# L0 attention of a four-stage kernel: projections moved by half a batch in four pieces, group sums in one bank pair, quantising in two parts, new first loads

## What is computed

```python
x = x + tanh(g_xattn[0]) * L0_xattn(layernorm(x), ctx, ctx)     # causal, 16 heads of 32, no weights
x = x + tanh(g_ffn[0])   * L0_ffn(layernorm(x), w_gate_up, w_proj)
x = x + tanh(g_xattn[1]) * L1_xattn(layernorm(x), ctx, ...)     # its keys and values: ctx @ k_w + k_b, ctx @ v_w + v_b
x = x + tanh(g_ffn[1])   * L1_ffn(layernorm(x), ...)
# L0_ffn's weights, in groups of 64:
scale = clip(mean(abs(w)), 1e-8); w_hat = clip(round(w / scale), -1, 1) * scale
# L1_ffn's weights: one scale for each matrix, from the mean of abs(w)
```

## Time and profile before

| | us |
|---|---|
| median of 3 runs | 1223.16 (1221.94 to 1225.69) |
| the profiled execution's own time | 1224.48 |
| its span | 1222.7 |
| TensorE busy in the span | 1131.6 (93%) |
| VectorE, ScalarE, GpSimd busy | 832.7, 567.3, 72.8 |

### The profile page before, as it was taken

One profiled execution on the slowest core, in us unless ns is written; L12 is line 12 of the kernel. 1 busy time (PEld: TensorE's weight loads), 2 busy tenths in 40 slices (PEclk: granted clock), 3 DMA queues, 4 the chain that ended last, 5 costly groups with the idle time before them and its releaser, 6 DMA issues.

```text
span 1222.7 us, 23942 instructions
## 1 busy us (share of the span) xinstructions
PE 1131.6 (93%) x9578; PEld 689.9 (56%) x9672; DVE 832.7 (68%) x1440; ACT 567.3 (46%) x918; POOL 72.8 (6%) x180
## 2 busy tenths in 40 slices
PE   4998999898989999999999897999999999999998
PEld 2555555555567777777777554545454545454543
DVE  5577767765756765755665545778787878777785
ACT  4655565656333332333333333336373737372644
POOL 0000000000000000000000010110101010101010
PEclk8999999999999999999999998999999999999999
DMA  9345434541131101111101020010101010100000
GB/s 359 125 132 174 156 121 130 166 147 61 44 121 53 51 29 36 53 35 35 53 18 35 18 78 23 15 35 2 52 2 52 2 52 2 35 10 10 10 9 35
DMA packets 28974, 78.75 MB, mean 64 GB/s; under 512 B 3009, under 2 KB 3137, under 8 KB 28481
## 3 DMA queue, kind: packets, MB, share of 16 engines
q1 hardware_dynamic: 28864, 77.22, 19.4%
HBM read 64.63 MB, written 12.58 MB: 63 GB/s over the span
## 4 chain that ended last, share of the span: by engine, by line
PE 84%; DVE 6%; ACT 4%; issue 4%; DMA 0%; POOL 0%; SPq 0%; ACTq 0%; DVEq 0%; POOLq 0%
PE bank L507 9%; PE bank L601 9%; PE bank L602 9%; PE bank L636 9%; PE bank L616 9%; PE bank L739 7%; PE bank L727 5%; PE bank L405 5%; PE bank L769 4%; PE bank L689 2%; PE bank L708 2%; PE bank L445 2%; ACT ARENA L965 2%; PE bank L466 2%; PE bank L421 2%
## 5 line engine op out<-in xcount | busy, mean ns | idle before, releaser
L601 PE MATMUL bank<-ARENA,W 128*128 128x256 f16 x1024 | 227.9, 273 | 0.9 <-issue 0.9
L602 PE MATMUL bank<-ARENA,W 128*128 128x256 f16 x1024 | 227.8, 273 | 0.0
L934 ACT ACTIVATE ARENA<-bank 128x512 f32<-128x512 f32 (+3 forms) x143 | 93.0, 687 | 107.0 <-PE bank L405 34.0
L739 PE MATMUL bank<-W,ARENA 128*128 128x512 bf16 x493 | 117.2, 383 | 4.7 <-ACT ARENA L934 2.2
L616 PE MATMUL bank<-W,ARENA 128*128 128x512 bf16 x472 | 116.3, 383 | 3.2 <-DVE ARENA L1347 0.9
L507 PE MATMUL bank<-ARENA 128*128 128x512 f32 x256 | 117.2, 602 | 0.0
L636 PE MATMUL bank<-ARENA 128*128 128x512 f32 x256 | 116.8, 599 | 0.0
L601 PEld LDWEIGHTS bank<-ARENA,W 128*128 128x128 bf16 x1024 | 100.4, 98 | 19.5 <-issue 1.3
L602 PEld LDWEIGHTS bank<-ARENA,W 128*128 128x128 bf16 x1024 | 100.5, 98 | 18.6 <-issue 0.3
L1486 DVE SCALAR_TENSOR_TENSOR ARENA<-bank,ARENA 128x512 f32<-128x512 f32 x64 | 48.0, 750 | 86.5 <-PE bank L602 86.5
L934 ACT ACTIVATE ARENA<-ARENA 128x512 f16<-128x512 f32 x64 | 40.3, 629 | 133.9 <-DVE ARENA L1486 131.1
(11 more groups left out here) (178 smaller groups left out, 1784.8 us busy)
## 6 DMA issues: line engine op xcount, KB each, us to landing
W<-in_w SPq DMA_DIRECT2D x48, 512.0 KB, 3.8
ARENA<-in_w SPq DMA_DIRECT2D x24, 512.0 KB, 3.6
kv_store<-ARENA SPq DMA_DIRECT2D x32, 256.0 KB, 2.2
W<-kv_store SPq DMA_DIRECT2D x15, 512.0 KB, 4.5
X<-in_x SPq DMA_DIRECT2D x8, 512.0 KB, 4.7
ARENA<-in_ctxT SPq DMA_DIRECT2D x8, 512.0 KB, 3.8
ARENA<-in_ctx SPq DMA_DIRECT2D x8, 512.0 KB, 6.1
out<-X SPq DMA_DIRECT2D x16, 256.0 KB, 2.9
```

The source lines that it names most:

```text
L601: pe.matmul(bank[:, i * S:(i + 1) * S], W0[:, at:at + P], xt_half(b, 0)[:, k, :], start=(k == 0), stop=False)
L602: mm = pe.matmul(bank[:, i * S:(i + 1) * S], W0[:, at:at + P], xt_half(b, 1)[:, k, :], start=False, stop=(k == KD - 1))
L739: mm = pe.matmul(to, bufC["QQ"][:, t, k * P:(k + 1) * P], W1[:, at:at + D], start=(k == 0), stop=(k == KD - 1))
L934: return act.activation(to, src, ACT.Copy)
```

## The change

Stage A is put in another order; no operation of the computation is dropped or added. Names as before; the new line numbers are some 3 to 20 higher.

- Key pieces 0 and 1 of batch f are made in the turn before that of the batch's attention, one after `a_turn_x(f)` and one between the last two `a_probs`; value pieces 2 and 3 stand after the first `a_scores` and after the second group sum's place in the batch's own turn. Turn 0 becomes a short lead-in of its own, with both key pieces of batch 0. Banks: `bank_of_kv` is 4, 1, 6, 7.
- The first group sum of a batch stays in the turn before, the second and third are in the batch's turn, all in banks 2 and 3.
- `a_quantise` becomes `a_distance` (four operations) and `a_ternary` (two, with the maximum). The first unit is quantised whole between the maxima of scores 0 and of scores 1; unit 1 has other work between its parts.
- In the last turn the first half of `b_gate_up(0, 0)` stands between the last two `a_probs`, the other half after `m_weights`.
- The first loads are `cst`, x, keys, `gate`, `cols`, then the key weights; `selq` and `selc` get a semaphore of their own and are copied after `split_row`. Stores of pieces 0 and 1 are issued at the end of the turn before.

```diff
-        kv = [[(f"kv{i}", s.a_kvr, 4, i, late)] for i in range(4)]
-        gs = [("gs0", s.a_s, 3, 0, 0), ("gs1", s.a_s, 3, 1, 0), ("gs2", s.a_s, 3, 2, late)]
+        kv = [[(f"kv{i}", s.a_kvr, 4, i, late * (i // 2))] for i in range(4)]
+        gs = [("gs0", s.a_s, 3, 0, 0), ("gs1", s.a_s, 3, 1, late), ("gs2", s.a_s, 3, 2, late)]
...
+        bank_of_kv = (4, 1, 6, 7)
...
+            sp.dma_start(pre["cst"], cst).then_inc(s.ld_cst, 16)
             load_x(0)
-            sp.dma_start(pre["cst"], cst).then_inc(s.ld_cst, 16)
-            sp.dma_start(pre["selq"], selq).then_inc(s.ld_cst, 16)
-            sp.dma_start(pre["selc"], selc).then_inc(s.ld_cst, 16)
+            load_keys(0)
             sp.dma_start(keep["gate"], gates).then_inc(s.ld_cst, 16)
             sp.dma_start(keep["cols"], cols).then_inc(s.ld_cst, 16)
-            load_keys(0)
+            sp.dma_start(bufA["wkv"][:, 0, :], wkv[:, 0:KD * D]).then_inc(s.ld_wk, 16)
+            sp.dma_start(bufA["tmp"][:, 0, :], vec[:, 0:D]).then_inc(s.ld_kb, 16)
             load_w0(0)
+            sp.dma_start(pre["selq"], selq).then_inc(s.ld_sel, 16)
+            sp.dma_start(pre["selc"], selc).then_inc(s.ld_sel, 16)
+            sp.dma_start(bufA["wkv"][:, 1, :], wkv[:, KD * D:2 * KD * D]).then_inc(s.ld_wv, 16)
...
+            a_project(0, 0, 0)
+            a_turn_x(0, 0)
+            a_group_sum(0, 0, 0)
+            a_project(0, 0, 1)
...
             for turn in range(NB + 1):
...
                 if back:
                     a_scores(b, 0)
+                    a_distance(b, 0)
+                    a_ternary(b, 0)
+                    a_scores(b, 1)
+                    a_max_parts(b, 0)
...
                     a_scores(b, 2)
-                    a_quantise(b, 1)
+                    a_distance(b, 1)
                 if end:
                     a_divide(e)
                 if back:
                     a_scores(b, 3)
                     a_max_parts(b, 1)
+                    a_ternary(b, 1)
                     if not front:
                         b_turn_x(0)
                     a_max_rows(b, 1)
-                    a_quantise(b, 2)
+                    a_distance(b, 2)
+                    a_ternary(b, 2)
```

More of the change, by code:

```diff
@@ L350, in sync_program @@
                 load_w0(3 * turn + 4)
[L351 to L352 removed]
+                if f < NB:
+                    store_kv(f, 0)
+                    store_kv(f, 1)
                 load_keys(turn + 1)
@@ L501, in a_project @@
                 what, t = i // TB, i % TB
-                bank = banks[(6, 7, 4, 5)[i]]
+                bank = banks[bank_of_kv[i]]
                 W = bufA["wkv"][:, what, :].rearrange("p (k d) -> p k d", k=KD)
-                pe.wait_ge(s.ld_wkv, 32)
-                pe.wait_ge(*ringA[(6, 7, 4, 5)[i]].freed(f"kv{i}", turn))
+                pe.wait_ge((s.ld_wk, s.ld_wv)[what], 16)
+                pe.wait_ge((s.ld_kt0, s.ld_kt1)[b % 2], 16 * (b // 2 + 1))
+                pe.wait_ge(*ringA[bank_of_kv[i]].freed(f"kv{i}", turn))
                 for k in range(KD):
@@ L531, in b_turn_x, with b_gate_up @@
                     turned(to, [bufB["xn"][:, t, k * P:(k + 1) * P] for k in range(KD)], keep["identf"]).then_inc(s.b_xt, 1)
-            for turn in range(NB + 1):
+            def b_gate_up(b, p, parts=(0, 1)):
+                q, first = 8 * b + p, 2 * ((p + 1) % 2)
+                if p == 0:
+                    pe.wait_ge(s.b_xl, 2 * b + 2)
+                if q == 0:
+                    pe.wait_ge(s.a_r, 16)
+                    pe.wait_ge(s.a_scr, 4 * NB)
+                if q == 1:
+                    pe.wait_ge(s.m_scl, 1)
+                    pe.wait_ge(s.a_otr, 3 * NB - 2)
+                pe.wait_ge(s.b_sg, max(0, q - 1))
+                pe.wait_ge(s.b_h, max(0, q - 1))
+                for part_ in parts:
+                    bank, col, done = banks[first + part_], part_ * HID + 2 * p * P, (s.b_g, s.b_gu)[part_]
+                    for i in range(2):
+                        for k in range(KD):
+                            at = k * 2 * HID + col + i * P
+                            pe.matmul(bank[:, i * S:(i + 1) * S], W0[:, at:at + P], xt_half(b, 0)[:, k, :], start=(k == 0), stop=False)
+                            mm = pe.matmul(bank[:, i * S:(i + 1) * S], W0[:, at:at + P], xt_half(b, 1)[:, k, :], start=False, stop=(k == KD - 1))
+                    mm.then_inc(done, 1)
@@ L534, in tensor_program @@
+            a_project(0, 0, 0)
+            a_turn_x(0, 0)
+            a_group_sum(0, 0, 0)
+            a_project(0, 0, 1)
+            for turn in range(1, NB + 1):
                 f, b, e = turn, turn - 1, turn - 2
-                front, back, end = f < NB, b in range(NB), e in range(NB)
-                if back:
-                    a_scores(b, 0)
+                front, end = f < NB, e >= 0
+                a_scores(b, 0)
+                a_project(turn, b, 2)
                 if end:
                     a_weigh(turn, e, 1)
-                if back:
-                    a_scores(b, 1)
+                a_scores(b, 1)
@@ L584, in m_weights @@
                 mm.then_inc(s.m_tot, 1)
-            def b_gate_up(b, p):
-                q, first = 8 * b + p, 2 * ((p + 1) % 2)
-                if p == 0:
-                    pe.wait_ge(s.b_xl, 2 * b + 2)
-                if q == 0:
-                    pe.wait_ge(s.a_r, 16)
-                if q == 1:
-                    pe.wait_ge(s.m_scl, 1)
-                    pe.wait_ge(s.a_otr, 3 * NB - 2)
-                pe.wait_ge(s.b_sg, max(0, q - 1))
-                pe.wait_ge(s.b_h, max(0, q - 1))
-                for bank, col, done in ((banks[first], 2 * p * P, s.b_g), (banks[first + 1], HID + 2 * p * P, s.b_gu)):
-                    for i in range(2):
-                        for k in range(KD):
-                            at = k * 2 * HID + col + i * P
-                            pe.matmul(bank[:, i * S:(i + 1) * S], W0[:, at:at + P], xt_half(b, 0)[:, k, :], start=(k == 0), stop=False)
-                            mm = pe.matmul(bank[:, i * S:(i + 1) * S], W0[:, at:at + P], xt_half(b, 1)[:, k, :], start=False, stop=(k == KD - 1))
-                    mm.then_inc(done, 1)
             def b_project(b, p):
```

166 lines of the change are left out of this document (83 added, 83 removed).

## The result

| | before | after |
|---|---|---|
| median of 4 runs each, us | 1222.55 (1221.92 to 1225.69) | 1202.39 (1200.88 to 1204.64) |
| ratio, 95% interval | | 0.9832 (0.9806 to 0.9858) |
| the profiled execution, its span | 1224.48, 1222.7 | 1204.64, 1202.8 |
| start of scores 0 of turn 1 | 17.23 | 27.07 |
| turn 1 | 41.75 | 38.68 |

20.2 us faster where 15 were forecast, so 1202.4 lies just under the range that began at 1203. The last sums came 14.3 us earlier, at 333.0, where 332 was forecast: stage A did nearly what the working said. The other 5.6 us of the profiled pair came behind stage A, where the forecast had the work shift unchanged. That 14.3 lies so near the 15.3 of the sum is partly luck: the start came out 3.0 us worse, turn 7 0.4 and the last turn 1.0; turn 1 came out 1.4 better and turns 2 to 6 2.1.

The account below looks back on a forecast made before the run. TensorE's work and its few waits bound the kernel. Start +6.8, turn 1 -1.7, turns 2 to 6 -9.7, turn 7 -2.7, last turn -8.0 sum to -15.3, taken as -15: 1208.2 us, range 1203 to 1217.

Parts of the forecast that it names:

- The three new waits: TensorE in a repeated turn: 1.5 us before the group sum, 0.6 before scores 3, 0.45 before probabilities 2.
- the 1.47, 0.71, 0.44 and 0.30: Old TensorE waits (us) before output transposes, last probabilities, weighing and scores 1 in each repeated turn, claimed to go.
- a pair of probabilities' work 1.72 (four): TensorE's cost for one pair of probabilities, start to start: 1.72 us, four times in a turn.
- 14.8, and 15.1 on TensorE: Lead-in: `split_row`, needed by key piece 0's bias, ends on VectorE at 14.8 us; TensorE has it at 15.1.
- I take 24.0 for a stretch at the lower clock: Start of scores 0 of turn 1: 23.6 us by the steps, taken as 24.0; before it was 17.23.
- The row says otherwise and I go by it: Lead-in: first products taken at full clock, 3.43 us for key piece 0; half clock would make the sum 2.3 worse.
- the price list: TensorE's steps in a repeated turn, each costed from start to start, summing to 35.9 us of the 40.44.
- only move: Last turn: the half of `b_gate_up` was said only to move, within a forecast gain of 8.0 us.
- Stage B is all matmuls and starts earlier by that: Behind stage A: the work shifts unchanged, starting earlier by stage A's gain, taken as 15 us.
- Half: Rival: clock falls at the start and in turn 1, costing 10 us instead of 2.7; 1215.5 us, chance 17%.
- nothing: Rival: VectorE's chain is longer than its rows, turns keep some 40.4 us; 1220 us, chance 6%.
- slower: Rival: clock falls at the 1.5 us wait in each of seven turns, 5 us more each; 1243 us, chance 5%.

Follow-up runs that it names:

- out_first: Changed kernel with the transposes of the output ahead of scores 3 again: 1209.03 us, ratio 0.9877 to the kernel before.
- key_together: Changed kernel with key piece 1 right behind key piece 0: 1210.61 us, ratio 0.9887 to the kernel before.
- unit0_behind: Changed kernel with the whole first unit back behind the maxima of scores 1: 1224.0 us, ratio 1.0005 to the kernel before.
- before_whole: Kernel before with only the first unit moved whole between the maxima of scores 0 and scores 1: 1255.58 us, ratio 1.0258.
- leadin_best: Changed kernel, lead-in reordered (group sum, x transposes before key bias; signs first), small loads right behind `cst`, first unit split in batch 0 alone: 1197.9 us, ratio 0.9795.
- seam_undone: Changed kernel with both halves of `b_gate_up(0, 0)` behind `m_weights` again: 1206.78 us, ratio 0.9879 to the kernel before.
- pad8: Changed kernel with 8 idle products (1.8 us) put into `m_weights`, between stages A and B: 1203.98 us.
- pad65: Changed kernel with 65 idle products (14.3 us) put into `m_weights`, between stages A and B: 1217.09 us.
- filled: Changed kernel with 26 idle products (12, 6 and 8) at three places at the head of layer 1: 1205.23 us, ratio 0.9852.
- filled_x: Changed kernel with idle products at the head of layer 1, 17 between the halves of the x transposes, then 6 and 8: 1207.07 us, ratio 0.9873.

## Why the prediction was right and wrong

- **Order of events, right.** The three new waits stand at the places named, two of them for what was named; the 1.47, 0.71, 0.44 and 0.30 went. `out_first` brings the 1.47 back and `key_together` the 0.71. `unit0_behind` and `before_whole` each undo one half of the exchange between TensorE and VectorE, and a longer wait comes in its place (2.3 and 3.9 us).
- **A turn of 38.5, was 38.08.** Along the walk: the group sum at 10.55 (forecast 10.5), scores 3 at 20.47 (20.8), the end at 38.08 (38.5). The largest term that was mis-sized is "a pair of probabilities' work 1.72 (four)": three of the four cost 1.55 to 1.57 here. Where the 1.72 was read, the row of the first four matmuls is 0.76 us long, and it is 0.60 here; a hidden wait for the copied maxima would explain that, but no row shows it. A sixth group sum half of 0.22 in the list, of which there is no record, makes another 0.2. A key piece between probabilities goes the other way (3.76 instead of 3.65). In all 0.42 a turn, 2.1 us in turns 2 to 6.
- **The start, +6.8 forecast, +9.8 in this profile** (24.2 to 27.07 in executions with the same lead-in, against 24.0 forecast). Two steps: "14.8, and 15.1 on TensorE" for the bias (16.55), since VectorE saw its constants at 8.10 us and not at 6.45 as before; and "I take 24.0 for a stretch at the lower clock", which allowed 0.4 where key piece 1 alone lost 1.5. The 2.26 us wait of the group sum stood as forecast in kind. In ten of twelve executions with this lead-in the clock did not fall there, so for most of them 24.0 was near.
- **The first products.** "The row says otherwise and I go by it" was wrong: key piece 0 took 5.22 us although the granted clock of that stretch reads 1.00. By the Trainium skill ("TensorE: Matmul & The Clock Gate", What's actually happening) the very first products run at 1.2 GHz, and the trace agrees: 5.22 and, in `leadin_best`, 5.97 us for work that takes 3.43 later. It could have been read in the kernel before as well. TensorE's first rows there:

```profile
12.05 1.94 PE L405 MATMUL bank<-ARENA 128*128 128x128 f32 x8 [12.05 <-DVE ARENA L1308]
13.78 1.91 PE L518 MATMUL bank<-W,ARENA 128*128 128x512 bf16 x4
```

  The eight transposes take 1.73 us from start to start, where the price list has 0.93 for the same work in a turn. In the change most of it was hidden by the wait for the bias, of which 0.96 was left. `before_whole` shows that the column can stay wrong for long: its first products take 5.89 us to their bias at 35.64 us, far into the program, and the column reads 1.00.

```profile
28.00:32.00 4.00, 2.67 (x4) 1.47 (x6) 2.98 (x9) 1.95 (x3) 0.69 (x1) 1.00 0.46 174
```

```profile
29.75 6.05 PE L507 MATMUL bank<-ARENA 128*128 128x512 f32 x8
35.64 0.38 PE L510 MATMUL bank<-ARENA 128*128 128x512 bf16 x1
```

- **Turn 1, -1.7 forecast, -3.1 measured.** The wait before the group sum was right (4.4 forecast, 4.31 measured), and 2.3 for the clock was near the 1.7 measured; the rest is the 0.4 of every turn and work that was costed too high.
- **Turn 7, -2.7 forecast, -2.3; last turn, -8.0 forecast, -7.0.** The wait of 2.0 at probabilities 2 was put at 2.7. What was left out is that the clock can fall behind it (0.57 over 324 to 328 us), while half of `b_gate_up` is in work, some 1.7 us. In the repeat it did not fall and the last turn gave -8.6, so 8.0 lies between the two. `seam_undone` shows that this half is cover too, and does not "only move".
- **Behind stage A: the step that failed.** "Stage B is all matmuls and starts earlier by that" carries everything behind stage A over unchanged and puts a change in its time at the lower clock at nothing; the "2 of clock" in the range was all the room for it. Stage A gave 14.3 of the 15.3 in the sum and 5.6 more came from the rest; in the repeated pair 16.1 and 2.8. The work there is constant to 1.8 us, but the time at the lower clock in it is not: 5.5 to 13.7 us in these profiles. The profile that the forecast was made against held 13.7, with `key_together` the most of all, and its repeat 8.5.

  It is not only a matter of single executions: the medians differ by 20.2 and 22.9 us in two sets of runs. How those split is not known, since each kernel was profiled twice. By an estimate stage A gives 16 to 18 us in most executions (the last sums lie at 329.4 to 330.8 in `pad8`, `pad65`, `filled` and `filled_x`, idle products taken off, against 347.3), which leaves 2 to 7 for the rest.

  That the changed kernel as a rule has less time at the lower clock there is not shown, and why it should stays open; position in time does not explain it (`pad65`), nor was it mended by products in the waits. The mean granted clock of an execution can't settle it either: of the kernel before, executions with 0.989 took 1219.8 to 1220.0 or 1225.4 to 1226.6, those with 0.993 took 1221.3 to 1222.4. A slow start that the column misses, as in `before_whole`, would explain that; no such execution of the kernel before was profiled.
- **The rivals.** Half, nothing and slower did not come. Slower was a real mechanism, at 3.9 us of waiting (`before_whole`), not at 1.05. By the Trainium skill (the same page, A second HAM failure mode: psum-queue depth-cycling) short idling between groups of matmuls makes the clock cycle; in the repeated turns here the 1.05 to 1.5 us waits left it at 1.00 in all but one turn (`out_first`), those of 3.9 us and more never did.
- **Loads at nothing** held: no wait for a load shows between 59 and 343 us.

## What to carry to other kernels

Two moves that are each worthless or harmful can be the gain together: delaying work on one engine pays only if as much work is put in front of whoever waits for it, so walk both engines through a whole turn before judging either move. When a step is priced start to start, take a place where the next step was ready, or a hidden wait may go into the price. And a profile is one execution: sum its time at the lower clock, stage by stage, repeat it before the forecast, and let the range hold the spread. Here the same work behind stage A took 868 to 876 us, and the miss below the range was 0.6.

## What the runs showed of the hardware

- The first float32 products ran at about half rate for most of their length while the granted clock of the stretch read 1.00 (5.2 to 6.6 us for 3.43 at the full clock). In `before_whole` this lasted to beyond 30 us into the program. Up to the first change that the column shows it is no evidence; the distance of the rows is.
- The clock fell behind every wait of 3.9 to 4.3 us in stage A (15 waits, in the group sum of turn 1 and in the turns of `before_whole`). Shorter ones are a matter of chance here: the 2.0 us wait before probabilities 2 of the last turn brought it down in 7 of 16 profiles, the 2.3 us one of `unit0_behind` in 1 of 5 turns, the 1.48 us one in 1 of 28. At the head of layer 1 it fell although the 2.05 us wait just ahead had been filled.
- Between executions of one kernel the turns repeat to 0.04 us and the 862 us behind stage A to about 1. What spreads in the profiled ones is the lead-in, and where and how long the clock is low, most of it in layer 1.
